# Row maxima of two heads at once in two row groups, with both maxima tiles of a key tile placed ahead of its scores

## The reference

```python
tokens = x.reshape(B, C, N).transpose(0, 2, 1)
qkv = (tokens @ w_proj + b_proj).reshape(B, N, 8, 96)
q, k, v = jnp.split(qkv, 3, axis=-1)
attn = jax.nn.softmax(jnp.einsum('bihd,bjhd->bijh', q, k) * 32 ** -0.5, axis=2)
out = jnp.einsum('bijh,bjhd->bihd', attn, v).reshape(B, N, 256) @ w_out + b_out + tokens
...
```

## Time and profile before

| | us |
|---|---|
| median of 3 runs | 2838.7 (2837.37 to 2839.07) |
| the profiled execution | 2838.16 |
| its span | 2836.4 |
| PE busy | 2652.5 (94%) |
| DVE busy | 1983.4 (70%) |
| ACT busy | 1286.8 (45%) |
| POOL busy | 698.3 (25%) |

### The profile page before, as it was taken

One profiled execution on the slowest core, in us unless ns is written; L12 is line 12 of the kernel. 1 busy time (PEld: TensorE's weight loads), 2 busy tenths in 40 slices (PEclk: granted clock), 3 DMA queues, 4 the chain that ended last, 5 costly groups with the idle time before them and its releaser, 6 DMA issues.

```text
span 2836.4 us, 44487 instructions
## 1 busy us (share of the span) xinstructions
PE 2652.5 (94%) x15932; PEld 1852.8 (65%) x15932; DVE 1983.4 (70%) x2297; ACT 1286.8 (45%) x1874; POOL 698.3 (25%) x444
## 2 busy tenths in 40 slices
PE   5899999999999999999999999999999999999994
PEld 4457775577656776567755777557775577656772
DVE  2665777666976768766786677766787666876666
ACT  2463435533365434644346343563435534364334
POOL 0440025300372014600236002540035300361011
PEclk7899999999999999999999999999999999999997
DMA  5300023000410005000050002300032000500016
GB/s 127 71 1 16 12 65 77 17 1 12 105 38 17 1 12 112 31 17 1 30 124 2 17 12 51 91 12 5 12 73 69 17 1 12 112 31 1 1 62 275
DMA packets 46238, 123.51 MB, mean 44 GB/s; under 512 B 9905, under 2 KB 21425, under 8 KB 42417
## 3 DMA queue, kind: packets, MB, share of 16 engines
q1 hardware_dynamic: 46000, 120.36, 15.9%
HBM read 41.96 MB, written 23.86 MB: 23 GB/s over the span
## 4 chain that ended last, share of the span: by engine, by line
PE 71%; issue 9%; DVE 6%; ACT 4%; SPq 4%; POOL 3%; DMA 2%; DVEq 0%; ACTq 0%; POOLq 0%
PE tile L1542 21%; PE pv L1542 11%; PE pv L1666 8%; PE tile L1628 7%; PE tile L1656 6%; PE tile L1801 4%; PE tile L1692 4%; SPq L582 3%; PE pv L1656 2%; PE tile L1823 2%; PE tile L1852 2%; DMA stack<-qk_r 1%; ACT p L854 1%; POOL qk_r L687 1%; PE tile L1720 1%
## 5 line engine op out<-in xcount | busy, mean ns | idle before, releaser
L1123 DVE TENSOR_REDUCE small<-tile 128x1 f32<-128x1024 f32 x512 | 600.0, 1216 | 130.8 <-PE tile L1628 128.2
L854 ACT ACTIVATE p<-tile 128x512 f32<-128x512 f32 (+1 forms) x632 | 405.2, 692 | 239.2 <-PE tile L1656 214.4
L745 POOL TENSOR_TENSOR row_sum<-act 128x256 f32<-128x256 f32 x32 | 41.6, 1318 | 1475.8 <-DVE act L1316 1475.8
L1542 PE MATMUL tile<-qk_r 128*128 128x512 f32 x1536 | 378.0, 395 | 0.0
L1628 PE MATMUL tile<-stack 96*128 96x512 f32 x1024 | 344.7, 436 | 19.9 <-DMA stack<-qk_r 14.9
L715 POOL TENSOR_TENSOR acc<-acc,p 128x1024 f32<-128x1024 f32 x144 | 339.2, 2385 | 4.1 <-ACT p L854 3.9
L1542 PEld LDWEIGHTS tile<-qk_r 128*128 128x128 f32 x1536 | 287.4, 188 | 66.2 <-issue 7.7
L1321 DVE TENSOR_TENSOR pl<-p,ph 128x1024 fp32r<-128x1024 f32 x128 | 158.2, 1236 | 220.8 <-ACT p L936 220.8
L1628 PEld LDWEIGHTS tile<-stack 96*128 96x128 f32 x1024 | 178.7, 192 | 188.3 <-issue 118.9
L1656 PE MATMUL tile<-stack 112*128 112x512 f32 x760 | 269.6, 420 | 24.9 <-ACT p L854 18.4
L1666 PE MATMUL pv<-p,v 128*32 128x512 f32 x2048 | 273.1, 610 | 1.4 <-ACT p L854 1.4
(11 more groups left out here) (286 smaller groups left out, 4507.2 us busy)
## 6 DMA issues: line engine op xcount, KB each, us to landing
stack<-qk_r SPq DMA_DIRECT2D x192, 256.0 KB, 5.0
x_in<-in_x_dram SPq DMA_DIRECT2D x8, 1024.0 KB, 5.0
act<-in_x_dram SPq DMA_DIRECT2D x8, 1024.0 KB, 4.9
x_scratch<-act SPq DMA_DIRECT2D x7, 1024.0 KB, 4.0
z_scratch<-act SPq DMA_DIRECT2D x7, 1024.0 KB, 3.9
stack<-ones SPq DMA_DIRECT2D x16, 256.0 KB, 4.7
w3f<-w3f_scratch SPq DMA_DIRECT2D x8, 512.0 KB, 3.3
fin_rest<-z_scratch SPq DMA_DIRECT2D x3, 1024.0 KB, 8.5
```

The costliest lines, as they stand in the source:

```text
L854: sc.activation(p0[:, jt % DEPTH, pair, first:first + len(heads) * HALF], tile_wait(batch, "st0", *u, jt, k), ACT.Exp, scale=float(D) ** - ...
L1123: ve.tensor_reduce(maxima[:, h * NT + it:h * NT + it + 1], t, X, ALU.max).then_inc(vector_done, vector.one("max0", g, h, it))
L1542: ins = mm(out, lhs[a][kt_], rhs[c][kt_], start=first and kt_ == 0 and m == 0, stop=last and kt_ == n - 1 and m == 2)
```

## The change

- An `s0` tile becomes two matmuls of 32 rows: two heads of a pair, each against one half of the keys, from the high parts only. The two stand in different row groups of the array. `ROWS` places the three pairings of each head in `stack` such that head h has its high parts in row group h. For the units' first group and half, `s0` reads `qk_r` itself and doesn't wait for the copies.
- `max0` reduces such a tile to two numbers a row; one small reduction (`max_both`) joins the halves. The negation goes into the spread (`minus8`, and a factor of -1 in `spread`), the low part goes. Head 3 has its maxima in 32 rows, the others in 16, so `key_ones` becomes two copies.
- `key_tile` puts both `s0` ahead of the four scores in every key tile of the looped units.
- In the head the `s0` tiles go in pairs, and the steps of layer 3 between them move by one at most; `qk0(1, 1)` stands ahead of `s0` 6 and 7. Three more warming matmuls stand in the first key tile of an image.
- In layers 1 and 2 the negation is written in place, with no copy.

```diff
 def key_tile(g, half, jt):
...
     if next_unit(g, half):
-        return ("s0", 0), ("st0", 0), ("st0", 1), ("s0", 1), ("st0", 2), ("st0", 3)
+        return ("s0", 0), ("s0", 1), ("st0", 0), ("st0", 1), ("st0", 2), ("st0", 3)
...
+ROWS = ((0, 1, 2), (1, 0, 2), (2, 0, 1), (3, 0, 1))
+IMAX_OF = (96, 96, 96, 64)
+NMAX_OF = (NMAX, NMAX, NMAX, 2 * NMAX)
...
                 def s0(g, h, it):
-                    if it == 0 or it == HT:
-                        pe.wait_ge(stacked[g][h], 48 * batch_of(("s0", g, h, it)) + 48)
+                    pair, part = divmod(h, 2)
+                    ahead = of_head(("s0", g, h, it))
+                    if ahead and (h, it) == (0, 0):
+                        scalar_wait("qk0_hi", 1, 0)
+                    elif not ahead and it % HT == 0 and part == 0:
+                        for q in range(2):
+                            pe.wait_ge(stacked[g][2 * pair + q], 48 * batch + 48)
                     o = free("s0", g, h, it)
-                    for s in halves:
-                        ins = mm(o[:, s], stack[0:IMAX, g, 0, h, it * P:(it + 1) * P], stack[0:IMAX, g, 1, h, s],
-                                 start=True, stop=True)
+                    for q in range(2):
+                        rows = slice(D * (2 * pair + q), D * (2 * pair + q) + D)
+                        i = slice(it * P, (it + 1) * P)
+                        queries, keys = ((qk_r[rows, g, t, 0, n] for t, n in ((0, i), (1, halves[part]))) if ahead else
+                                         (stack[rows, g, t, 2 * pair + q, n] for t, n in ((0, i), (1, halves[part]))))
+                        ins = mm(o[:, halves[q]], queries, keys, start=True, stop=True)
...
                 def max_rows(g, half):
-                    negate((g, half), G, ts, ("max0", *rows_of((g, half), G * HT - 1)))
+                    own("max0", *rows_of((g, half), G * HT - 1))
+                    ve.tensor_reduce(maxima.rearrange("p (h t) -> p h t", h=G)[:, :, ts], parts0[:, :, ts], X, ALU.max
+                                     ).then_inc(vector_done, vector.one("max_both", g, half))
...
-                    if head and k == 7:
+                    if head and k == 6:
                         qk0(1, 1)
...
                     if head:
                         s0(*rows_of(UNITS[0], k))
+                        s0(*rows_of(UNITS[0], k + 1))
...
+                            if u == UNITS[0] and jt == 0 and (kind, k) == ("s0", 1):
+                                if body:
+                                    pe.wait_ge(scalar_done, scalar.at(b, "z_kept", 1))
+                                warm(pv[:, HALF:N], 3)
```

More of the change, by code:

```diff
@@ L208, in vector_steps @@
         s += [("max0", *rows_of(UNITS[0], k))]
-    s += [(n, *UNITS[0]) for n in ("neg_hi", "neg_copy", "neg_lo")]
-    s += [("max_rows", *UNITS[0], h) for h in range(G // 2)]
+    s += [("max_both", *UNITS[0])]
+    s += [("max_rows", *UNITS[0], h) for h in VECTOR_ROWS]
     for u in UNITS:
@@ L221, in vector_steps @@
         if following:
-            s += [(n, *following) for n in ("neg_hi", "neg_copy", "neg_lo")]
-            s += [("max_rows", *following, h) for h in range(G // 2)]
+            s += [("max_both", *following)]
+            s += [("max_rows", *following, h) for h in VECTOR_ROWS]
     s += [("stat", 1, 0, ct) for ct in range(CT)]
@@ L245, in of_head @@
         return name[1] == 0 and name[3] < HT
-    if kind in ("m0", "neg_hi", "neg_copy", "neg_lo", "max_rows", "max_cols"):
+    if kind in ("m0", "max_both", "max_rows", "max_cols"):
         return unit == UNITS[0]
@@ L253, in of_first_layer @@
     kind = name[0]
-    if kind in ("neg_hi", "neg_copy", "neg_lo"):
-        return len(name) == 3
     return kind in ("stat", "out0", "s0", "st0", "m0", "pv0", "den0", "ex0", "exp0", "max_cols", "pv0_out", "res_hi",
-                    "max0", "max_rows", "add0", "rec0", "rows0", "res", "res_lo", "x1") and (kind, name[1]) not in (
+                    "max0", "max_both", "max_rows", "add0", "rec0", "rows0", "res", "res_lo", "x1") and (kind, name[1]) not in (
                         ("stat", 2), ("stat", 3))
@@ L1122, in max0, with negate, spread @@
                     t = tile_wait("s0", g, h, it)
-                    ve.tensor_reduce(maxima[:, h * NT + it:h * NT + it + 1], t, X, ALU.max
+                    pair, part = divmod(h, 2)
+                    ve.tensor_reduce(parts0[:, 2 * pair:2 * pair + 2, it, part], t.rearrange("p (q n) -> p q n", q=2), X, ALU.max
                                      ).then_inc(vector_done, vector.one("max0", g, h, it))
[L1126 to L1142, removed]
+                def negate(layer):
+                    own("max", layer, NT - 1)
+                    hi = negmax[:, 0]
+                    TS(hi.bitcast(F32R), maxima[:, 0:NT], -1.0, None, ALU.mult).then_inc(vector_done, vector.one("neg_hi", layer))
+                    own("neg_hi", layer)
+                    STT(negmax[:, 1], maxima[:, 0:NT], -1.0, hi, ALU.mult, ALU.subtract
+                        ).then_inc(vector_done, vector.one("neg_lo", layer))
+                def spread(dst, src, mask, sign=1.0):
+                    rows, n = mask.shape
+                    return STT(dst.rearrange("p (t n) -> p t n", t=n),
+                               src.rearrange("p (a n) -> p a n", a=1).broadcast_to((rows, n, P)), sign,
+                               mask.rearrange("p (t a) -> p t a", a=1).broadcast_to((rows, n, P)), ALU.mult, ALU.mult)
                 def add0(u, jt, pair):
@@ L1160, in max_rows @@
                     ts = slice(half * HT, (half + 1) * HT)
[L1161 removed]
+                    own("max0", *rows_of((g, half), G * HT - 1))
+                    ve.tensor_reduce(maxima.rearrange("p (h t) -> p h t", h=G)[:, :, ts], parts0[:, :, ts], X, ALU.max
+                                     ).then_inc(vector_done, vector.one("max_both", g, half))
                     t = tile_wait("m0", g, half)
[L1163 to L1164 removed]
+                    for k, h in enumerate(VECTOR_ROWS):
+                        rows = slice(IMAX_OF[h], IMAX_OF[h] + NMAX_OF[h])
+                        spread(stack[rows, g, 0, h, half * HALF:(half + 1) * HALF], t[0:NMAX_OF[h], k * P:(k + 1) * P],
+                               ident[0:NMAX_OF[h], TURNED[h] + ts.start:TURNED[h] + ts.stop], -1.0
                                ).then_inc(vector_done, vector.one("max_rows", g, half, h))
@@ L1949, in turn @@
                     qk0(0, 1, (0,))
-                for k in range(G * HT):
-                    if body and k == 1:
+                for k in range(0, G * HT, 2):
+                    if body and k == 2:
                         mt_tile()
```

74 lines of the change are left out of this document (43 added, 31 removed).

## The result

The changed kernel takes 2926.35 us (median of 4 runs, 2915.92 to 2934.63) against 2838.68 us (2837.37 to 2839.07): a ratio of 1.0308, 95% interval 1.0268 to 1.0348. The forecast was 2860 us, the range 2828 to 2905. The sign was right, and the size was not: 3.1% slower instead of 0.8%. The profiled execution took 2919.89 us, its span is 2918.1 us, 81.7 us more than before.

A forecast was written before the change was run, and what follows sets the result against it. TensorE was busy 94%, but ScalarE's exponential was taken to set the score block, hiding the second maxima tile. Loops +45, image's start -12, first turn -8 and clock -3 gave +22 on 2838.2: 2860 us, range 2828 to 2905.

The forecast's parts named there:

- Loops, +45: In the 24 looped units, both maxima tiles ahead of the scores lengthen key tiles: +45 us (40.6 + 4.7).
- S: Time in a key tile that maxima work takes ahead of the first score: 0.78 us forecast, 0.57 before with one tile.
- both holds in key tiles 1 and 2: Second maxima tile waits for VectorE's maximum, then `res`, delaying the first score: +0.94 for key tiles 0 and 1, +1.01 for 2.
- the first rival: Switching the array from row groups to scores is free, or half so: 2828 us, chance 0.15.
- the second: Rival: the two row-group matmuls of a maxima tile run in turn, not together: 2924 us, chance 0.12.
- halving the maxima: Rival: TensorE's work sets the key tile, so halved maxima matmuls are the gain: 2725 us, chance 0.04.
- The clock in the loops, chance 0.05: Rival: TensorE waits more in the loops, so its clock falls once a unit, 1.7 us each: +41, 2903 us.
- The image's start, -12: Products before the copies start earlier in turns after the first: 1.65 us in each of 7 images, -12 us.
- First turn, -8: First maxima no longer wait for copies, so `qk0(1,1)` comes earlier in the first turn: -8 us (bounds -7 and -10).
- Clock behind the copies, -3: TensorE's shorter wait for copies in key tile 2 loses less clock afterwards: -3 us (bounds 0 and -5).
- Layers 1 and 2, costed at nothing: One 0.18 us copy goes, 16 times: at most 3 us, counted as nothing since the values' product runs beside it.
- Warming matmuls, costed at nothing in place: Three matmuls (0.9 us) in an image's first key tile lie beside ScalarE's `max_cols`: nothing; uncovered, 7 us in all.

The follow-up runs named there:

- fourth run: The changed kernel with both 32-row matmuls of a maxima tile in the same row group: 3007.68 us, ratio 1.0593.
- fifth run: The changed kernel with the second maxima tile back between second and third score, and GpSimd's low part waiting for VectorE's small operations: 2848.15 us, ratio 1.0037.
- second run: The kernel before with both maxima tiles ahead of the scores in every key tile, nothing else changed: 2906.38 us, ratio 1.0245.
- first run: The changed kernel with the loop order of the kernel before, second maxima tile between second and third score: 2873.43 us, ratio 1.0157.
- the best kernel: The changed kernel with GpSimd's later start and both maxima tiles between third and fourth score in key tiles 1 to 7: 2808.67 us, ratio 0.9903.
- ninth run: The best kernel with both maxima tiles between third and fourth score in key tile 0 too, save an image's first unit: 2833.63 us, ratio 0.9991.
- third run: The changed kernel with GpSimd's first low part of an image waiting until VectorE's small operations are over: 2892.85 us, ratio 1.0209.
- the tenth: The kernel before, without row groups, with both maxima tiles between third and fourth score in key tiles 1 to 7: 2842.44 us, ratio 1.0017.

## Why the prediction was wrong

- **Loops, +45.** The mechanism and its sizes hold: S = 0.77 (0.66 and 0.11 of bare load) where 0.78 was forecast, 3.28 us for 3.30, +2.3 us a unit for +2.54, both holds in key tiles 1 and 2. In a unit without a fall of the clock (1557.61 to 1590.53), against one of before, key tiles 0 and 1 take 0.88 more (0.94 forecast), key tile 2 0.93 more (1.01), each middle one 0.19 more (0.21), and key tile 7 0.27 less (0.25). The third change of division costs what the other two did, so the first rival falls; row groups run together (fourth run), so the second falls; and halving the maxima gave nothing where the forecast said that they cost nothing (fifth run). In the first unit the difference is +0.5 where the landing of before had no fall of the clock behind it (0.59 forecast).
- **The clock in the loops, chance 0.05.** This step failed: the sum put it at nothing. Fourteen of the 16 units have a fall, near 2 us each and 28 in all. (That rival's own sum is 2 too high: 2860 and 41 are 2901.) The reason given against it, waits that grow by tenths, was drawn from one middle key tile. In key tiles 0 to 2 several waits stand together, 1.0 us in the stretch behind a unit's first denominator product. The windows view has this stretch at full clock, for a unit in which the clock falls right behind it and for one in which it does not fall, and below for a unit of the second run, where no unit has a fall:

```profile
1172.50:1181.40 8.90, 7.90 (x145) 5.42 (x144) 6.51 (x7) 4.75 (x11) 1.04 (x1) 1.00 0.03 12
1557.60:1566.50 8.90, 7.90 (x145) 5.44 (x144) 6.49 (x7) 4.75 (x11) 1.04 (x1) 1.00 0.01 2
```

```profile
1168.50:1177.40 8.90, 8.17 (x145) 6.16 (x144) 6.46 (x7) 4.71 (x11) 1.04 (x1) 1.00 0.01 3
```

With the old order the units' falls are gone (first run), with the order of the best kernel all but one in 16, and with waits of 0.42 and 0.48 us in key tiles 0 and 1 (the second is one of a weight load) they are back in 9 of 16 (ninth run). So in the changed kernel the order of the loop brings the falls and takes them away. But the second run has the same order, most of the waits, slower maxima and no fall. Which wait decides, and why two units were spared with the same 7.90 us of work behind them, is not shown.
- **The image's start, -12.** This is the step that failed by as much: +16, 28 us off. The chain of the forecast is right (without the hold -1.5 in one head of the changed kernel and in those of the third run). Left out was what the earlier start meets: `qk_full` ends earlier, and GpSimd's operation starts beside VectorE's small ones. In the kernel before they stood half a us apart:

```profile
1092.63 0.15 DVE L1436 TENSOR_TENSOR pairs<-pairs 128x2 f32<-128x2 f32 x1
...
1093.16 2.36 POOL L687 TENSOR_TENSOR qk_r<-qk_full,qk_r 128x1024 fp32r<-128x1024 f32 x1 [6.32 <-ACT qk_full L826]
```

The hold was one small shift away. The third run shows the hold, with the half clock behind it, as the cause: without it the heads take 26 us less. The Trainium skill, "SBUF — State Buffer", "SBUF: two separate sides", says that GpSimd and a VectorE operation with two inputs in SBUF exclude each other for the whole instruction, whichever starts first. The trace agrees on the block (2.34 us beside 2.35), and the recorded starts are too close to show which was first. The sum should have asked for it where an edit moves one of the two.
- **First turn, -8:** -7.1. **Clock behind the copies, -3:** about right in the later images; the three of before in which the landing was followed by 21.2 us instead of 19.7 have 20.2 now. The first image still loses the clock there.
- **Layers 1 and 2, costed at nothing:** +8.0, in small steps all along 194 us: twelve equal matmuls take 2.92 us instead of 2.88, with TensorE busy and at full clock. Before, and after:

```profile
1275.04 2.88 PE L1542 MATMUL tile<-qk_r 128*128 128x512 f32 x12
```

```profile
1312.17 2.92 PE L1559 MATMUL tile<-qk_r 128*128 128x512 f32 x12
```

Every kernel made from the changed one has it (194.6) and none made from the one before (193.6 in the second run, 193.5 in the tenth), on the same chip too. Its cause was not tried and stays open.
- **Warming matmuls, costed at nothing in place:** right as to their own time, but they pay 10 us by the clock, which the forecast did not count. Without them the changed kernel would presumably have been slower still; that was not run.

## What to carry to other kernels

Work with a price of its own (here two changes of the array's division) belongs inside an existing wait, and once only: two row-group products together, in front of the score that waits anyway, turn +3.1% into -1.0%, with GpSimd's wait. When an edit lets a step start earlier, look at what it will then stand beside: a GpSimd operation that began with VectorE's small ones cost 5.5 us a time here, and starting it a quarter of a us later took that away. And do not cost waits singly on TensorE: where several short ones came to stand together, 28 us of lost clock came on top of the 37 that they and the array's changes cost themselves. Taking work off the engine may be part of that: here the loops with the faster maxima lost the clock, and the same order with the slower ones did not.

## What the runs showed of the hardware

- Two 32-row matmuls in different row groups take one pitch of 0.23 us; in the same group two (0.66 and 1.12 us for four, up to the next score). Entering and leaving the division costs two tenths of a us, and a pair alone takes 0.43.
- A VectorE operation with both inputs in SBUF on 128 x 2 numbers took 2.34 us, held for the length of a GpSimd operation that began 0.02 us earlier. In other heads, with the same 0.02 us, it took 0.15.
- Three matmuls that compute nothing, ahead of a wait, kept 15 us of one image at full clock (1.00 against 0.77) and gave 10 us in eight images.
- A fall of the clock in a loop cost 1.5 to 3.7 us a unit, and the same group of eight values' matmuls takes 1.94 us in it instead of 1.06.
